# Key and query loads stacked into fewer transfers, and the first loads of a four-layer kernel put in another order

## The chip, the core and the metric

The kernel runs on one core of one Trainium2 chip. Its time is the device time of one execution in microseconds (us). The kernel before takes 3858.27 us, the median of 3 runs (3856.71 to 3861.03). The core has TensorE (PE, with its weight loads shown as PEld), VectorE (DVE), ScalarE (ACT), GpSimd (POOL) and SyncE (SP), and 16 DMA engines that all the engines' queues share. SP does nothing here but wait and start transfers.

## The reference, cut to what matters

Four layers work on one sequence x of 2048 tokens of 256 numbers. Each layer adds a cross attention over a context of 1601 rows of 192 numbers, and then a feed-forward part with routed experts.

```python
x = x + _L0_xattn_ref(_layernorm(x), ctx, Wq, bq, Wkv, bkv, Wo, bo)   # 16 heads of 16
x = x + _L0_ffn_ref(_layernorm(x), ...)        # 16 experts + shared, top 4
x = x + _L1_xattn_ref(...)                     # 16 heads of 16
x = x + _L1_ffn_ref(...)                       # 8 experts, top 2, gelu
x = x + _L2_xattn_ref(...)                     # 8 heads of 32
x = x + _L2_ffn_ref(...)                       # 8 experts, top 2, linear
x = x + _L3_xattn_ref(..., mask, ...)          # 16 heads of 16, the only one with the mask
x = x + _L3_ffn_ref(...)                       # 16 experts, top 2, gated

# one attention:
q, k, v = x @ Wq + bq, ctx @ Wk + bk, ctx @ Wv + bv      # split into heads
out = softmax(q @ k.T * scale) @ v
return out @ Wo + bo
```

All is float32. The scores are made of bfloat16 products: each query and key is split into three bfloat16 parts that add up to it, and six products of parts are summed.

## The kernel before, in words

**Stacks.** For a head of 16 numbers the six products are one matmul with 6 x 16 = 96 rows of contraction: `KS` (`k_stack`) holds for each head the key parts 0, 1, 0, 2, 1, 0 one under the other, each on 16 partitions, and `QS` (`q_stack`) the query parts that go with them, 0, 0, 1, 0, 1, 2. `PRODUCTS` is the list. For layer 2 with heads of 32 a stack is two halves of three parts each. A row 96 carries ones or the mask, rows 96 to 99 the negative row maxima.

**How a stack is filled.** The projections come out of PE with the channels on the partitions. ACT copies them, POOL or DVE splits them into three parts in a staging buffer `QP` (two of them, used in turn for keys and queries; a buffer is free when its store has landed), and SP stores them into DRAM (`k_parts`, `q_parts`, three parts of 256 channels each). From there `load_keys` and `load_queries` bring them back, each part onto its 16 (or 32) partitions of the stack. The heads are in four groups (g 0 to 3). `load_keys` issues six transfers of 200.1 KB for a group, 16 partitions x 4 heads x 1601 numbers. `load_queries` issues six of 64 KB and one for the row of ones, for a group and a chunk of 512 tokens.

**Maxima and scores.** Before the softmax of a group can start, the row maxima are needed: PE makes the scores of 128 tokens against 400 keys (L2259), DVE reduces them (L1524). Then in 13 steps over the keys PE makes the scores again (L2295), ACT takes the exponential (L1257), PE multiplies with the values (L2309), and maxima of the groups to come are made beside it. In steady state 16 groups of one layer (4 chunks x 4 groups) follow each other like this.

**The opening of layer 0.** SP loads x's first chunk, the context, all attention weights, then after a fence (all engines meet) the other chunks of x and the constant rows of the stack. ACT issues, beside it, the mask and the gate weights, with elements of 1 byte to 128 bytes. PE projects keys 0 to 2, turns the first tokens, and makes key 3 and queries 0 and 1 (`FIRST_UNITS`). When all their stores have landed, SP loads queries (0,0), keys of group 0, queries (0,1), keys of group 1; it stores the queries of groups 2 and 3, waits until that has landed, and loads queries (0,2). Then it stores keys 4 to 7 as they come. DVE turns the mask into numbers (`masks`). PE then works off 89 jobs of maxima (`side_prologue`), and after every second one a piece of the rest of the projections (`behind`): keys 4 to 7, values, the turning of the tokens ("turn"), queries. PE takes both in this one order, so a piece that waits holds back the maxima behind it.

**Layers 1 and 3** get their stacks during the feed-forward part before them: POOL issues the 24 key loads, one each time PE has finished a further unit (`load_keys(pool, ...)`), and SP stores and loads the first queries (`first_queries`). **Layer 2** gets them after layer 1's feed-forward part, from SP.

Lines to follow: L467 `load_keys`, L551 and L556 `load_queries`, L533 `store_query_parts`, L524 `store_key_parts`, L513 constant rows, L504 the attention weights but the key's, L608 x, L1100 to L1110 mask and gates on ACT's queue, L1139 ACT's copy of a key projection, L2324 "turn", L2155 the first half of a key projection on PE.

Of the kernel before, what the change touches and what calls it, by code (L numbers as in the profile page):

```python
# [5 lines left out]
T, D, S, DC = 2048, 256, 1601, 192  # L6
P = 128
# [30 lines left out]
PRODUCTS = [(0, 0), (1, 0), (0, 1), (2, 0), (1, 1), (0, 2)]  # L38
# [127 lines left out]
def build(nc, A, out):  # L166
# [5 lines left out]
    q_parts = nc.dram_tensor("q_parts", [3, D, T], bf16, kind="Internal").ap()  # L172
    k_parts = nc.dram_tensor("k_parts", [3, D, S], bf16, kind="Internal").ap()
# [8 lines left out]
    with ctx:  # L182
# [163 lines left out]
        s_wa = sem("s_wa")  # L346
        s_stat = sem("s_stat")
# [111 lines left out]
        def load_keys(eng, L, g, rows=(0, 6)):  # L459
# [11 lines left out]
        def _(sp):  # L471
# [12 lines left out]
            def load_attention_weights(L):  # L484
                a = ATT[L]
                dh, pw, hpg = a["dh"], a["pw"], a["hpg"]
                H = D // dh
                n = 0
# [5 lines left out]
                for dst, src in keys:  # L494
                    sp.dma_start(dst, src).then_inc(s_wk, 16)
                loads = [(WQ[:], A[f"wq{L}"].rearrange("(k p) n -> p k n", p=P)),
                         (WV0[:], A[f"wv{L}"][0:P, :]), (WV1[0:DC - P, :], A[f"wv{L}"][P:DC, :])]
                loads.append((WO[:], A[f"wo{L}"].rearrange("(a p) n -> p a n", p=P)))
                if L < 3:
                    loads += [(BQ[:], A[f"bq{L}"].rearrange("(m p) -> p m", p=P)),  # L500
                              (WV1[DC - P:DC - P + 1, :], A[f"bv{L}"].rearrange("(a n) -> a n", a=1)),
                              (BO[:], A[f"bo{L}"].partition_broadcast(P))]
                for dst, src in loads:
                    sp.dma_start(dst, src, allow_slow_non_contiguous=True).then_inc(s_wa, 16)  # L504

# [10 lines left out]
            def store_key_parts(u):  # L516
# [6 lines left out]
                dst = k_parts[:, m * P:(m + 1) * P, c * Q:c * Q + n].rearrange("r p t -> p r t")  # L523
# [3 lines left out]
            def store_query_parts(c, m):  # L527
# [4 lines left out]
                dst = q_parts[:, m * P:(m + 1) * P, c * Q:(c + 1) * Q].rearrange("r p t -> p r t")  # L532
# [8 lines left out]
            def load_queries(L, t, buf):  # L541
# [6 lines left out]
                if a["nsub"] == 1:  # L548
                    for row, (_, part) in enumerate(PRODUCTS):
                        src = q_parts[part].rearrange("(h d) t -> d h t", d=dh)[:, g * hpg:(g + 1) * hpg, cols]  # L550
                        sp.dma_start(dst[row * dh:(row + 1) * dh, :, :], src).then_inc(s_ql[buf], 16)  # L551
                else:
                    for row, (_, part) in enumerate(PRODUCTS):
                        src = q_parts[part].rearrange("(h d) t -> d h t", d=dh)[:, g * hpg:(g + 1) * hpg, cols]
                        r = row % 3
                        sp.dma_start(dst[r * dh:(r + 1) * dh, row // 3::2, :], src).then_inc(s_ql[buf], 16)  # L556
# [45 lines left out]
            sp.dma_start(X[:, 0:TPQ, :], x_chunks[0]).then_inc(s_x0, 16)  # L602
            sp.dma_start(C0[:], A["ctx_t"][0:P, :]).then_inc(s_ctx, 16)
            sp.dma_start(C1[0:DC - P, :], A["ctx_t"][P:DC, :]).then_inc(s_ctx, 16)
            load_attention_weights(0)
            fence(sp, fences)
            for c in range(1, NQ):
                sp.dma_start(X[:, c * TPQ:(c + 1) * TPQ, :], x_chunks[c]).then_inc(s_in, 16)  # L608
            load_constant_rows(0)
# [7 lines left out]
            load_keys(sp, 0, 0)  # L617
# [2200 lines left out]
```

## Time and profile before

| | |
|---|---|
| median of 3 runs | 3858.27 us (3856.71 to 3861.03) |
| the profiled execution | 3857.22 us, its span 3855.5 us, mean granted PE clock 0.966 |
| PE busy | 3615.5 us, 94% |
| DVE busy | 2536.7 us, 66% |
| ACT busy | 1931.5 us, 50% |
| POOL busy | 645.9 us, 17% |
| DMA | 171.33 MB, mean 44 GB/s |

A row of the stages (windows) view gives, for a stretch of the span, each engine's busy time and in brackets its instructions, the granted clock of PE, the mean busy share of the 16 DMA engines and what they moved. A row of the timeline is start, duration, engine, line, what is written from what, a count, and in square brackets the idle time just before it with what ended it. The duration of a transfer on SPq, ACTq or POOL is the time to issue it, from the first to the last of the count, and not the transfer itself.

### The profile page before, as it was taken

The numbers are of one execution on the slowest core, as the hardware profiler recorded it, in microseconds if no ns is written. First come the engines' busy times: TensorE is split into PE (matmuls) and PEld (weight loads), VectorE is DVE, ScalarE is ACT, GpSimd is POOL, SyncE is SP. The second block draws the span as 40 slices with busy tenths as digits, with TensorE's granted clock in tenths as the row PEclk, the third lists the DMA queues.
The fourth block names the chain that finished last, engine by engine and source line by source line (L and its number), as shares of the span: only waits on it lengthen the run. The fifth ranks groups of instructions, "written<-read, shape, count | busy, mean of one in ns | idle before, by whom it ended". The sixth has DMA issues, their size and how long they took to land. (4 is left out here: it accounts for less than half of the span.)

```text
span 3855.5 us, 50411 instructions
## 1 busy us (share of the span) xinstructions
PE 3615.5 (94%) x17554; PEld 1563.8 (41%) x17555; DVE 2536.7 (66%) x5373; ACT 1931.5 (50%) x2358; POOL 645.9 (17%) x940
## 2 busy tenths in 40 slices
PE   5999999799999999987997899999799999998996
PEld 2333333365533333325665333333433333332564
DVE  5888888456678888844223655553478888884523
ACT  3677777521147777762332444444203777777111
POOL 3200001200041010014221301010313001001242
PEclk8999999899999999998999899999799999999998
DMA  6300000123000000025001400000140000001144
GB/s 129 54 19 16 17 18 6 50 75 77 24 30 15 18 14 19 9 65 202 31 30 50 114 20 16 18 18 5 58 94 31 18 18 15 18 10 49 53 121 133
DMA packets 132653, 171.33 MB, mean 44 GB/s; under 512 B 38379, under 2 KB 106589, under 8 KB 130257
## 3 DMA queue, kind: packets, MB, share of 16 engines
q1 hardware_dynamic: 119280, 142.27, 13.2%
q0 software_dynamic: 10144, 26.08, 2.7%
q8 instruction: 126, 2.06, 0.2%
q14 instruction: 95, 0.77, 0.1%
q10 hardware_dynamic: 3008, 0.15, 0.1%
HBM read 131.27 MB, written 40.84 MB: 45 GB/s over the span
## 5 line engine op out<-in xcount | busy, mean ns | idle before, releaser
L1524 DVE TENSOR_REDUCE mx<-ps 128x1 f32<-128x400 f32 (+1 forms) x3584 | 1818.4, 566 | 495.3 <-PE ps L2259 483.9
L1257 ACT ACTIVATE probs<-ps,zero_col 128x1024 f32<-128x1024 f32 (+1 forms) x1040 | 1111.1, 1111 | 585.0 <-PE ps L2295 584.6
L2259 PE MATMUL ps<-k_stack,q_stack 97*128 97x400 bf16 (+1 forms) x3584 | 1076.5, 339 | 50.1 <-DMA k_stack<-k_parts 27.8
L2295 PE MATMUL ps<-q_stack,k_stack 100*128 100x512 bf16 (+2 forms) x3328 | 1056.9, 381 | 6.4 <-ACT probs L1257 6.4
L2309 PE MATMUL ps<-probs,v 128*32 128x512 f32 (+2 forms) x5824 | 891.5, 607 | 0.2 <-ACT probs L1257 0.2
L2259 PEld LDWEIGHTS ps<-k_stack,q_stack 97*128 97x128 bf16 x3584 | 290.4, 97 | 1049.2 <-DVE mx L1524 624.8
L1257 ACT ACTIVATE probs<-ps,mask_col 128x1024 f32<-128x1024 f32 (+1 forms) x416 | 439.5, 1110 | 158.6 <-PE ps L2295 158.6
L2295 PEld LDWEIGHTS ps<-q_stack,k_stack 100*128 100x128 bf16 (+2 forms) x3328 | 323.3, 100 | 345.0 <-ACT probs L1257 65.8
L2309 PEld LDWEIGHTS ps<-probs,v 128*32 128x32 f32 (+2 forms) x5824 | 140.1, 111 | 264.3 <-issue 248.8
L1674 DVE SCALAR_TENSOR_TENSOR x_res<-ps,comb,x_res 128x256 f32<-128x256 f32 x336 | 148.1, 479 | 63.0 <-PE ps L2559 57.5
L1325 ACT ACTIVATE h_t_s<-ps 128x512 f32<-128x512 f32 x80 | 47.8, 597 | 254.3 <-PE ps L2550 254.3
L2559 PE MATMUL ps<-w_up_s,h_t_s 128*128 128x256 f32 x640 | 164.4, 387 | 6.7 <-DVE x_res L1674 3.4
L932 POOL TENSOR_TENSOR o_t<-o_sum,recip_wide 128x512 f32<-128x512 f32 x32 | 40.7, 1273 | 713.4 <-DMA recip_wide<-row_recips 713.4
L2550 PE MATMUL ps<-xn_t,w_up_s 128*128 128x512 f32 x320 | 150.3, 592 | 0.6 <-ACT v L1151 0.6
L2640 PE MATMUL ps<-w_all,xn_t 128*128 x624 | 144.5, 385 | 3.7 <-ACT xn_t L1339 2.4
L934 POOL TENSOR_TENSOR o_sum<-o_sum,recip_wide 128x512 f32<-128x512 f32 x28 | 35.8, 1277 | 648.2 <-DMA recip_wide<-row_recips 648.2
L2619 PE MATMUL ps<-w_all,xn_t 128*128 x312 | 142.3, 599 | 1.6 <-SPq L776 1.6
L2559 PEld LDWEIGHTS ps<-w_up_s,h_t_s 128*128 128x128 f32 x640 | 114.2, 189 | 58.4 <-DVE x_res L1674 26.3
L2640 PEld LDWEIGHTS ps<-w_all,xn_t 128*128 128x128 f32 x624 | 118.2, 192 | 42.6 <-issue 28.0
L1339 ACT ACTIVATE xn_t<-ps,tile_bias 128x128 f32<-128x128 f32 x312 | 84.7, 382 | 100.0 <-PE ps L2631 99.8
L1369 ACT ACTIVATE silu_gate<-ps 128x320 f32<-128x320 f32 (+3 forms) x60 | 28.1, 468 | 197.0 <-PE ps L2715 99.7
L2573 PE MATMUL ps<-w_up_s,xn_t 128*128 128x512 f32 x256 | 120.0, 612 | 0.5 <-DVE x_res L1918 0.5
(293 smaller groups left out, 2715.0 us busy)
## 6 DMA issues: line engine op xcount, KB each, us to landing
q_stack<-q_parts SPq DMA_DIRECT2D x384, 64.0 KB, 2.2
q_parts<-qk_part SPq DMA_DIRECT2D x32, 384.0 KB, 2.5
w_up<-in_up SPq DMA_DIRECT2D x17, 704.0 KB
w_up_s<-in_expert SPq DMA_DIRECT2D x40, 256.0 KB, 2.7
k_stack<-k_parts SPq DMA_DIRECT2D x48, 200.1 KB, 7.1
k_stack<-k_parts POOLq DMA_DIRECT2D x48, 200.1 KB, 4.1
k_parts<-qk_part SPq DMA_DIRECT2D x24, 384.0 KB, 3.1
w_all<-in_up SPq DMA_DIRECT2D x8, 1024.0 KB, 12.6
```

The source lines that it names most:

```text
L1257: act.activation(PR[pair[0] % 4][0:r, :, :], PS[0:r, 2 * b:2 * b + 2, :], ACT.Exp, bias=mask_col[0:r, k:k + 1] if L == 3 else zero_col[0:r ...
L1339: last = act.activation(HB[:, q * P:(q + 1) * P], PS[:, 2 + q // 4, q % 4 * P:(q % 4 + 1) * P], ACT.Gelu, bias=BT[:, bass.ds(i, 1), q], sc ...
L1524: ins = dve.reduce_max(MX4[g % 2][:, u, c:c + 1], PS[:, bank, 0:CK[c]], AX.X)
L1674: dve.scalar_tensor_tensor(X[:, t, :], PS[:, b, 0:D], c, X[:, t, :], ALU.mult, ALU.add).then_inc(s_yf, 1)
L2259: last = mm(PS[:, bank, 0:CK[c]], QS[g][0:97, slot_of(j), qt * P:(qt + 1) * P], KS[0:97, (g * hpg + j) * nsub, CKO[c]:CKO[c] + CK[c]], sta ...
L2295: last = mm(PS[0:r, b + i, :], KS[0:rows, (g * hpg + jj) * nsub + sub, k * P:k * P + r], QS[g][0:rows, slot_of(jj) + sub, :], start=sub == ...
L2309: last = mm(PS[pw * jj:pw * jj + pw, 4, :], V[0:r, k, (g * hpg + jj) * pw:(g * hpg + jj) * pw + pw], PR[used[0] % 4][0:r, i, :], start=k = ...
L2550: last = mm(PS[:, n % 2, :], up[:, k, :], xnT[:, k, c * Q:(c + 1) * Q], start=k == 0, stop=k == 1)
L2559: mm(PS[:, 2 + yj[0] % 3, 0:D], HTS[n % 2][:, 0, i * P:(i + 1) * P], weight_slot(load)[1], start=True, stop=True).then_inc(s_y, 1)
L2573: last = mm(PS[:, n % 4, :], xnT[:, k, t * P:(t + 1) * P], WUS[i % 2][:, k * 512:(k + 1) * 512], start=k == 0, stop=k == 1)
L2619: last = mm(PS[:, half, :], XT1[par][:, k * P:(k + 1) * P], w1.rearrange("p a f -> p (a f)"), start=k == 0, stop=k == 1)
L2640: last = mm(PS[:, 4 + par, 0:D], HB[:, q * P:(q + 1) * P], w2.rearrange("p a f -> p (a f)"), start=q == 0, stop=q == NF // P - 1)
```

## The change

- **Stacked loads.** The channels of `wq`, `wk`, `bq`, `bk` are permuted on the way in (`heads_last`), so that in `q_parts` and `k_parts` the parts of a head group lie at one stride: number d of all heads of a half stands together. A load then brings several parts of the stack at once: for keys `(row, n, part)` is 3 times part 0, 2 times part 1, once part 2, and the repeat is a leading dimension of step 0 in the source (`to_broadcast`); for queries it is parts 0, 1, 2, then 0, 1, then 0, at a step. So a key group is 3 transfers in place of 6, a query group 4 in place of 7. In layer 2 a key group is 4 (three of one part and one of parts 0, 1, 2), a query group 6 in place of 7. The bytes are the same. The destination of a head group's rows is contiguous too now: 6404 numbers in a run.
- **POOL's key loads** for layers 1 and 3 are 12, one after every second unit.
- **First loads.** Context and key weights go first, x's first chunk after them, then the query weights; the constant rows go ahead of the other chunks of x. The value weights (`wv`, `wo`, `bv`, `bo`) go behind the keys of group 0. Mask and gates leave ACT's queue and stand on SP's behind queries (0,2). There is a semaphore of its own for the query weights.
- **masks()** moves from DVE to POOL, between the splitting of key 7 and of the first queries.
- **lead**: in layer 2 the first piece of `behind` comes after six maxima and not after two.

```diff
-PRODUCTS = [(0, 0), (1, 0), (0, 1), (2, 0), (1, 1), (0, 2)]
+KEY_LOADS = {1: [(0, 0, 3, 0, 0), (0, 3, 2, 1, 0), (0, 5, 1, 2, 0)],
+             2: [(0, 0, 1, 0, 0), (0, 1, 1, 0, 0), (0, 2, 1, 1, 0), (1, 0, 3, 0, 1)]}
+QUERY_LOADS = {1: [(0, 0, 3, 0, 1), (0, 3, 2, 0, 1), (0, 5, 1, 0, 0)],
+               2: [(0, 0, 2, 0, 1), (0, 2, 1, 0, 0), (1, 0, 1, 2, 0), (1, 1, 1, 1, 0), (1, 2, 1, 0, 0)]}
...
+        def stacked(parts, L, g, load):
+            dh, hpg = ATT[L]["dh"], ATT[L]["hpg"]
+            _, _, n, part, step = load
+            rows = parts[g // 2].rearrange("r (d h) s -> (r d) h s", h=P // dh)
+            heads = slice(g % 2 * hpg, (g % 2 + 1) * hpg)
+            if step == 0:
+                src = rows[part * dh:(part + 1) * dh, heads, :]
+                return src.unsqueeze(0).to_broadcast([n] + list(src.shape)) if n > 1 else src
+            return rows[part * dh:(part + n) * dh, heads, :]
...
-            for i in range(*rows):
-                part, _ = PRODUCTS[i]
-                src = k_parts[part].rearrange("(h d) s -> d h s", d=dh)[:, g * hpg:(g + 1) * hpg, :]
-                r, sub = (i, 0) if nsub == 1 else (i % 3, i // 3)
-                eng.dma_start(KS[r * dh:(r + 1) * dh, 4 * g + sub:4 * g + 4:nsub, :], src).then_inc(done, 16)
+            for load in KEY_LOADS[nsub][slice(*loads)]:
+                sub, r, n = load[0:3]
+                dst = KS[r * dh:(r + n) * dh, 4 * g + sub:4 * g + 4:nsub, :]
+                eng.dma_start(dst, stacked(k_parts, L, g, load)).then_inc(done, 16)
...
             load_queries(0, (0, 0), 0)
             load_keys(sp, 0, 0)
+            load_value_weights(0)
             load_queries(0, (0, 1), 1)
             load_keys(sp, 0, 1)
             store_query_parts(0, 1)
             wait_landed(qd)
             load_queries(0, (0, 2), 2)
+            sp.dma_start(mask_u8[:, 0:NK - 1], ...).then_inc(s_mask, 16)      # and 9 more
...
-                    for i in range(6 * NG):
-                        pool.wait_ge(s_y, results.at() + per_unit * (begin + i))
-                        load_keys(pool, L + 1, i // 6, (i % 6, i % 6 + 1))
+                    for i in range(3 * NG):
+                        pool.wait_ge(s_y, results.at() + per_unit * (begin + 2 * i))
+                        load_keys(pool, L + 1, i // 3, (i % 3, i % 3 + 1))
...
+                lead = TPQ if L == 2 else 0
                 for n, job in enumerate(jobs):
                     side(job)
-                    if n % every == every - 1 and behind:
+                    if n >= lead and n % every == every - 1 and behind:
```

The order of instructions shows the three places. First, SP's queue at the start of the program, before: key bias, query and value weights, then behind the fence (`s_fence`) the other three chunks of x, the constant rows and the first key stores.

```order
L495 DMA wk<-in_bk 1x256
L504 DMA wq<-in_wq 128x2x256
L504 DMA wv<-in_wv 128x256
L504 DMA wv<-in_wv 64x256
L504 DMA wo<-in_wo 128x2x256
L504 DMA bq<-in_bq 128x2x1
L504 DMA wv<-in_bv 1x256
L504 DMA bo<-in_bo 128x256
L608 DMA x_res<-in_x 128x4x256 [waits s_fence]
L608 DMA x_res<-in_x 128x4x256 x2
L513 DMA k_stack<-const_rows 1x16x1601 x4
L524 DMA k_parts<-qk_part 128x3x512 [waits s_kp] x3
```

The same stretch now, from the program's first transfer on.

```order
L618 DMA ctx_a<-in_ctx_t 128x1601
L619 DMA ctx_b<-in_ctx_t 64x1601
L505 DMA wk<-in_wk 128x256 [waits s_wpad]
L505 DMA wk<-in_wk 64x256
L505 DMA wk<-in_bk 1x256
L621 DMA x_res<-in_x 128x4x256
L508 DMA wq<-in_wq 128x2x256
L510 DMA bq<-in_bq 128x2x1
L534 DMA k_stack<-const_rows 1x16x1601 [waits s_fence]
L534 DMA k_stack<-const_rows 1x16x1601 x3
L626 DMA x_res<-in_x 128x4x256 x3
```

Four transfers with 0.59 MB (value weights, `wo`, `bv`, `bo`) have left the stretch ahead of the first key store, and the first chunk of x stands behind the key weights.

Second, SP's queue from the loads of queries (0,0) on, before (`s_kd`, `s_qd`: the key and query stores have landed; `s_kp`, `s_qp`: parts are ready to be stored).

```order
L551 DMA q_stack<-q_parts 16x4x512 [waits s_kd1,s_kd0,s_qd1]
L551 DMA q_stack<-q_parts 16x4x512 x5
L557 DMA q_stack<-const_rows 1x16x128
L467 DMA k_stack<-k_parts 16x4x1601 x6
L551 DMA q_stack<-q_parts 16x4x512 x6
L557 DMA q_stack<-const_rows 1x16x128
L467 DMA k_stack<-k_parts 16x4x1601 x6
L533 DMA q_parts<-qk_part 128x3x512 [waits s_qp]
L551 DMA q_stack<-q_parts 16x4x512 [waits s_qd1]
L551 DMA q_stack<-q_parts 16x4x512 x5
L557 DMA q_stack<-const_rows 1x16x128
L524 DMA k_parts<-qk_part 128x3x512 [waits s_kp] x3
```

The same place now, down to the value weights.

```order
L572 DMA q_stack<-q_parts 48x4x512 [waits s_kd1,s_kd0,s_qd1]
L572 DMA q_stack<-q_parts 32x4x512
L572 DMA q_stack<-q_parts 16x4x512
L573 DMA q_stack<-const_rows 1x16x128
L481 DMA k_stack<-k_parts 48x1x6404
L481 DMA k_stack<-k_parts 32x1x6404
L481 DMA k_stack<-k_parts 16x6404
L520 DMA wv<-in_wv 128x256
L520 DMA wv<-in_wv 64x256
L520 DMA wo<-in_wo 128x2x256
L520 DMA wv<-in_bv 1x256
L520 DMA bo<-in_bo 128x256
```

Queries (0,1) and keys of group 1 follow in the same form. Third, what stands on SP between the store of the queries of groups 2 and 3 and the stores of keys 4 to 6, now.

```order
L554 DMA q_parts<-qk_part 128x3x512 [waits s_qp]
L572 DMA q_stack<-q_parts 48x4x512 [waits s_qd1]
L572 DMA q_stack<-q_parts 32x4x512
L572 DMA q_stack<-q_parts 16x4x512
L573 DMA q_stack<-const_rows 1x16x128
L641 DMA mask_u<-in_mask 128x12x1
L643 DMA mask_u<-in_mask 65x1
L645 DMA mask_row_u<-in_mask 1x1601
L648 DMA gate_w<-in_gw 128x2x32 x3
L651 DMA gate_b<-in_gb 128x8
L648 DMA gate_w<-in_gw 128x2x32
L651 DMA gate_b<-in_gb 128x16
```

The stores of keys 4 to 7 now come behind ten more transfers.

## Rows read from the trace of the kernel before

**Rows 1.** Stages of 60 us: busy per engine, PE's clock, DMA share, GB/s.

```profile
0.00:60.00 60.00, 18.92 (x43) 8.76 (x45) 26.99 (x71) 17.09 (x35) 13.43 (x19) 0.75 0.80 153
...
180.00:240.00 60.00, 60.00 (x366) 20.22 (x359) 53.31 (x110) 46.13 (x45) 5.34 (x10) 1.00 0.07 18
```

**Rows 2.** Timeline, layer 0's opening: what PE waited for.

```profile
54.45 0.83 PE L2259 MATMUL ps<-k_stack,q_stack 97*128 97x401 bf16 x2 [27.80 <-DMA k_stack<-k_parts]
...
70.40 0.33 PE L2155 MATMUL ps<-ctx_a,wk 128*128 128x65 f32 x2
...
74.92 0.66 PE L2324 MATMUL ps<-ident,probs 128*128 128x128 f32 x4 [1.35 <-ACT qk_part L1140]
```

**Rows 3.** Timeline, ACT in layer 0's opening: the copies of keys 2, 5, 6, 7.

```profile
29.72 0.60 ACT L1139 ACTIVATE qk<-ps 128x512 f32<-128x512 f32 x1 [7.45 <-DMA k_parts<-qk_part]
...
66.08 0.60 ACT L1139 ACTIVATE qk<-ps 128x512 f32<-128x512 f32 x1 [3.81 <-DMA q_parts<-qk_part]
...
72.50 0.60 ACT L1139 ACTIVATE qk<-ps 128x512 f32<-128x512 f32 x1 [5.00 <-DMA k_parts<-qk_part]
...
74.53 0.23 ACT L1139 ACTIVATE qk<-ps 128x65 f32<-128x65 f32 x1 [0.60 <-DMA k_parts<-qk_part]
```

**Rows 4.** Transfers of the first 60 us: GB/s in 40 slices of 1.5 us; ACT's queue.

```profile
GB/s 0 138 195 149 401 200 158 160 257 241 282 334 348 198 39 95 153 139 128 59 5 0 196 196 132 33 30 133 103 190 132 128 130 134 122 150 237 130 128 135
...
q10 hardware_dynamic: 3008, 0.15, 4.2%
```

**Rows 5.** Timeline, SP's queue in layer 0's opening.

```profile
39.24 2.69 SPq L551 DMA_DIRECT2D q_stack<-q_parts  x6
41.97 0.52 SPq L557 DMA_DIRECT2D q_stack<-const_rows  x1
42.53 2.92 SPq L467 DMA_DIRECT2D k_stack<-k_parts  x6
...
65.99 2.65 SPq L551 DMA_DIRECT2D q_stack<-q_parts  x6
68.68 0.50 SPq L557 DMA_DIRECT2D q_stack<-const_rows  x1
69.22 8.85 SPq L524 DMA_DIRECT2D k_parts<-qk_part  x4
```

**Rows 6.** Stages: loads to 128 partitions, constant rows to one, key loads to 16.

```profile
18.00:20.00 2.00, 2.00 (x3) 0.59 (x3) 1.74 (x3) 0.16 (x1) 0.00 (x0) 1.00 1.17 350
20.00:22.00 2.00, 2.00 (x12) 1.45 (x11) 0.74 (x2) 1.79 (x4) 0.00 (x0) 1.00 1.28 81
120.00:122.00 2.00, 2.00 (x7) 0.79 (x6) 1.81 (x4) 1.11 (x1) 2.00 (x4) 0.50 1.06 120
```

**Rows 7.** The page's list of transfers: count, size, median us from issue to landing.

```profile
q_stack<-q_parts SPq DMA_DIRECT2D x384, 64.0 KB, 2.2
```

**Rows 8.** Timeline, ACT's queue: mask and gates (first and last of 10).

```profile
1.01 0.44 ACTq L1100 DMA_DIRECT2D mask_u<-in_mask  x1
...
8.13 0.84 ACTq L1110 DMA_DIRECT2D gate_b<-in_gb  x1
```

**Rows 9.** Timeline, POOL between key 7's split and the first query.

```profile
81.34 1.15 POOL L864 TENSOR_TENSOR qk<-qk,qk_part 128x512 f32<-128x512 f32 x1 [3.65 <-ACT qk_part L1238]
```

**Rows 10.** Timeline, PE in layer 2's opening; SP and PE in layer 3's.

```profile
2147.00 1.12 PE L2324 MATMUL ps<-ident,probs 128*128 128x128 f32 x4 [2.96 <-ACT probs L1189]
2147.91 0.88 PE L2259 MATMUL ps<-k_stack,q_stack 97*128 97x400 bf16 x2
...
2831.28 0.85 SPq L533 DMA_DIRECT2D q_parts<-qk_part  x1
2838.30 3.85 SPq L551 DMA_DIRECT2D q_stack<-q_parts  x6
2842.19 0.56 SPq L557 DMA_DIRECT2D q_stack<-const_rows  x1
...
2844.40 1.16 PE L2259 MATMUL ps<-k_stack,q_stack 97*128 97x401 bf16 x3 [8.37 <-issue]
```

More of the change, by code:

```diff
@@ L547, in load_queries @@
                 dst = QS[buf]
[L548 to L556, printed above, removed]
+                for load in QUERY_LOADS[a["nsub"]]:
+                    sub, r, n = load[0:3]
+                    rows = dst[r * dh:(r + n) * dh, sub::a["nsub"], :]
+                    sp.dma_start(rows, stacked(q_parts, L, g, load)[:, :, cols]).then_inc(s_ql[buf], 16)
                 sp.dma_start(dst[96:97, :, :], ones_row).then_inc(s_ql[buf], 16)
@@ L622, in _ @@
             load_queries(0, (0, 2), 2)
+            sp.dma_start(mask_u8[:, 0:NK - 1], A["mask"][:, 0:P * (NK - 1)].rearrange("a (k p) -> p (a k)", p=P),
+                         allow_slow_non_contiguous=True).then_inc(s_mask, 16)
+            sp.dma_start(mask_u8[0:KREM, NK - 1:NK], A["mask"][:, P * (NK - 1):S].rearrange("a p -> p a"),
+                         allow_slow_non_contiguous=True).then_inc(s_mask, 16)
+            sp.dma_start(mask_row_u8[:], A["mask"]).then_inc(s_mask, 16)
+            for L in range(4):
+                E = FFN[L]["E"]
+                sp.dma_start(GW[:, L], A[f"gw{L}"].rearrange("(k p) e -> p k e", p=P),
+                             allow_slow_non_contiguous=True).then_inc(s_gl, 16)
+                if L >= 2:
+                    sp.dma_start(GB[:, L, 0:E], A[f"gb{L}"].partition_broadcast(P)).then_inc(s_gl, 16)
             def first_queries(L):
@@ L854, in link, with masks @@
                 pool.wait_ge(s_const, n[0])
+            def masks():
+                pool.wait_ge(s_mask, 3 * 16)
+                link(pool.memset(mask_col[:], 0.0))
+                for r, lo, hi in ((P, 0, NK - 1), (KREM, NK - 1, NK)):
+                    link(pool.tensor_copy(mask_col[0:r, lo:hi], mask_u8[0:r, lo:hi]))
+                    link(pool.tensor_scalar(mask_col[0:r, lo:hi], mask_col[0:r, lo:hi], 1.0, -MASKED,
+                                            ALU.subtract, ALU.mult))
+                link(pool.tensor_scalar(mask_row, mask_row_u8[:], 1.0, -MASKED, ALU.subtract, ALU.mult))
             def clear_attention_weights(L):
@@ L965, in _ @@
                             split_keys(u, staged.take("key")[0])
+                        masks()
                     pool.wait_ge(s_qp, qp.at())
@@ L971, in _ @@
                 if L < 3:
-                    wa.step(16 * 7)
+                    wa.step(16 * 5)
                     pool.wait_ge(s_wa, wa.at())
@@ L1099, in _ @@
             rs = Count(s_rs)
[L1100 to L1110 removed]
+            wq = Count(s_wq)
             fence(act, fences)
@@ L1165, in scale_bias @@
             def scale_bias(scale):
+                wq.step(32 if wq.n < 96 else 16)
+                act.wait_ge(s_wq, wq.at())
                 act.activation(BQS[:], BQ[:], ACT.Copy, scale=scale).then_inc(s_bq, 1)
@@ L1598, in _ @@
                     if L == 0:
-                        masks()
                         for u in range(4):
@@ L2178, in project_next @@
                     wk.step(16 * (3 if L < 3 else 2))
-                    wa.step(16 * (7 if L < 3 else 4))
+                    wq.step(16 * (2 if L < 3 else 1))
+                    wa.step(16 * (5 if L < 3 else 3))
                     pe.wait_ge(s_wk, wk.at())
@@ L2350, in _ @@
                     wk.step(16 * 3)
-                    wa.step(16 * 7)
+                    wq.step(16 * 2)
+                    wa.step(16 * 5)
                     pe.wait_ge(s_wk, wk.at())
@@ L2764, in pairs_of_groups, with heads_last @@
         return np.swapaxes(m, 1, 2).reshape(D, D)
+    def heads_last(m, dh):
+        m = m.reshape(*m.shape[:-1], 2, P // dh, dh)
+        return np.swapaxes(m, -1, -2).reshape(*m.shape[:-3], D)
     def contraction_first(m, n):
```

76 lines of the change are left out of this document (33 added, 43 removed).

## The prediction

> **What bounds the kernel now.** I read the stages first. In the middle of an attention PE is busy without a gap (60.00 of 60 us, clock 1.00) and the DMA engines are 7% busy [rows 1]: there a cheaper transfer is worth nothing, since no engine waits for one. What the change touches can count only in the openings. In the first 60 us PE is busy 18.9 us, and the DMA engines 80% [rows 1]. So I read that opening in the timeline, engine by engine.
>
> PE stands still from 26.65 to 54.45 us, until the keys of group 0 have landed [rows 2]. That wait is a chain: ACT copies key 2 at 29.72, when the store of key 0 has landed and freed its staging buffer [rows 3]; the last stores land and SP starts to load at 39.24; it issues seven query and six key loads until 45.45 [rows 5]. After that there is a second chain, which decides the end of the opening. The store of the queries of groups 2 and 3 stands in the queue behind group 1's keys and lands at 65.99, and only then ACT can copy key 5, at 66.08; SP loads queries (0,2), stores key 4 at 69.22 [rows 5], ACT copies key 6 at 72.50 and key 7 at 74.53 [rows 3], and PE, which has waited 1.35 us, goes on at 74.92 with the turning of tokens [rows 2]. From there the opening runs on work, not on transfers. So the question is when PE reaches this instruction in the changed kernel.
>
> **Durations of transfers.** The rate goes with the destination: x to 128 partitions runs at 350 GB/s, the constant rows to one partition at 81, the key loads to 16 partitions at 120, each with the DMA engines full [rows 6]. The best slice has 401 GB/s [rows 4], which is 25 GB/s for each of 16 engines.
>
> **Step 1, the first loads.** Ahead of the first key store stand 0.59 MB less (value weights, wo, bv, bo; shapes in the order), 1.7 to 4.9 us at 350 to 120 GB/s; I take 2.0, since these go to 128 partitions. The small packets of ACT's queue, 4.2% of 16 engines for 60 us [rows 4], are 2.5 us. The engines are full where rows 6 look into this time (shares 1.17 and 1.28), so both come off: ACT copies key 2 at 25.2 and the loads start at 39.24 - 4.5 = 34.7. That the first chunk of x comes later, and the constant rows before the other chunks, changes nothing in the sum of the bytes ahead of that store; bounds of this step 0 (if the chain on PE and DVE sets the store) and 7.4 us.
>
> **Step 2, issue.** Seven query loads take 2.69 + 0.52 = 3.2 us [rows 5], four 1.8. Their 0.46 MB at 120 to 350 GB/s land in 1.3 to 3.9 us, I take 2.3: key data of group 0 flow from 38.0.
>
> **Step 3, the stacked key loads.** This is the term on which all depends and the trace does not show it. A group is 1.23 MB (6 x 200.1 KB). Bounds: 3.1 us, with all engines at their best (401 GB/s), and 56 us, if few engines work at the 7.5 GB/s each that the key loads show (120 / 16). Two of the three new loads have a source whose leading dimension is the repeat, 3 or 2, and a destination of 48 or 32 partitions. A transfer that is dealt out to the engines along the leading dimension of both sides can be dealt to three and to two of them only. I take this as the likeliest: engines 0 and 1 then carry 205 KB of the first load, 205 KB of the second and 12.8 KB of the third, 0.423 MB at 25 GB/s = 16.9 us, against 10.2 us before (1.23 MB at 120). The rate of 25 and not 7.5, because what held the key loads to 120 is by rows 6 the few partitions written at a time, and runs of 12.8 KB in place of 3.2 can't cost more. The only repeated source in rows 6 is the constant rows', with 16 repeats, and the engines were full with it: a repeat as such doesn't confine, but this row can't show what three do.
> The Trainium skill, DMA: Bandwidth & Descriptors, section on why a DMA increments its semaphore by 16, says that the engine count is the largest one up to 16 that divides the slowest dimension of both access patterns, and its rules for authors warn of a leading zero-stride broadcast of c copies; by it the counts are 3, 2 and 16, and no run shown here tests that.
>
> Landing adds 2.2 us [rows 7]: keys of group 0 are there at 38.0 + 16.9 + 2.2 = 57.1, against 54.45. The 4.5 us of step 1 are gone.
>
> **Step 4, what is queued behind.** All later transfers on SP's queue use the loaded engines too: value weights (37 KB each at 25 GB/s, 1.5 us), queries (0,1) (28 KB, 1.1), group 1's keys (16.9), the query store (25 KB, 1.0). So it lands at 54.9 + 20.5 + 2.2 = 77.6, against 65.99. The value weights land 1.5 us behind group 0's keys, and PE asks for them only some maxima and a key projection later: no wait, and about 1 us if that cover is gone.
>
> **Step 5, SP's new duties.** Then 1.8 us of query loads and the ten transfers of mask and gates. On ACT's queue they took from 1.01 to 8.97 us, 8.0 us [rows 8]. ACT had nothing to do then; on SP the store of key 4 stands behind them. Bounds 4.5 us (ten at 2.69 / 6, what a query load takes to issue [rows 5]) and 8.0; I take 8.0, the row of the same transfers. Key 4 is stored at 77.6 + 1.8 + 8.0 = 87.4, against 69.22. As before ACT copies key 6 3.3 us after it and key 7 2.0 us later [rows 3, 5], and PE turns 0.4 us after that: 93.1, against 74.92, **18.2 us later**.
> PE takes its jobs in order, so the maxima behind can't fill this: it reaches the first half of key 7 (70.40, 16 us after its first maximum [rows 2]) at 73 us and stops there until key 5 is copied at 77.7.
>
> **Step 6, masks on POOL.** DVE loses work in a time in which it waits for PE's first maximum anyway: nothing. The long one of the six instructions is 1601 numbers on one partition; POOL's 512 on each partition take 1.15 us [rows 9], so 3.6 us, and POOL stands idle 3.65 us at that place. I take nothing; bounds 0 and +3.6, should the queries' split have to wait for all of it. SP issues the mask about 10 us before POOL gets there.
>
> **Step 7, the other openings.** Layer 2: PE waits 2.96 us for ACT with two maxima done; four more, twice 0.88 us by the next row, fit in [rows 10]: -1.5 us (bounds 0, -2.9). Layer 3: queries are stored at 2831.28, SP loads them from 2838.30 to 2842.75, and PE starts at 2844.40 after 8.37 us [rows 10]; four loads in place of seven save 1.8 us. But POOL's stacked key loads then run beside that store on two or three engines, and packets of 12.8 KB can hold it up: 0 to +8 us; I take 0. Layer 1's key loads come one after every second expert unit and expert weights are loaded four ahead: nothing, at most what I allow for layer 3. Layer 2's key loads have no repeat and are covered.
>
> **Sum.** +18.2 - 1.5 - 1.8 = +14.9 us. The profiled execution took 3857.22 us (span 3855.5 and 1.7 around it), 1.1 us under the median of the runs: 3872.1 for it, 3873 for a median.
>
> **Rivals.**
> (a) *The stacks use all 16 engines.* For it: the repeat of 16 in rows 6, and nothing in the trace against it. Then 1.03 MB to 48 and 32 partitions at 300 GB/s and 0.2 MB at 120 take 5.1 us. First maximum 38.0 + 5.1 + 2.2 = 45.3; query store landed at 43.1 + 2.0 + 1.5 + 5.1 + 1.3 + 2.2 = 55.2; SP 1.8 + 8.0: key 4 stored at 65.0, PE turns at 70.7, 4.2 us earlier. With step 7: -7.5 us, 3851; with the ten transfers at 4.5 us, 3847. This is the other side of zero.
> (b) *The stacks move as slowly as before* (destination-bound at 120 GB/s whatever their shape). Query store landed at 48.2 + 2.0 + 1.5 + 10.2 + 1.3 + 2.2 = 65.4; +9.8, +5.7: PE turns at 80.9, +6.0; with step 7 +2.7: 3861. The change then does little of what it says.
> (c) *Few engines, and something else gets stuck too*: the engine's rate is under 25 GB/s, or in layer 3 the query store waits its full 8 us behind POOL's packets. Each 5 GB/s less costs 4.2 us in each of two groups. From 3886 up.
>
> **Chances.** Forecast (3864 to 3886) 0.62; (a) 0.22; (b) 0.08; (c) 0.08. The forecast's own range is 3864 to 3886: 16.9 could be 14 or 20 us twice, step 5 3.5 us less, step 1 3 us either way. To hold 8 in 10 the range must reach into (a) and (c): 3850 to 3888. A measurement of this kernel can tell 0.2%, 7.7 us, from no change. Faster by more: half of (a) and a little, 0.12. Within: the rest of (a), (b), and the bottom of the forecast, 0.24. Slower: 0.64.
>
> **What would show it.** In the profile after: PE's first maximum (layer 0) at 57 if the forecast is right, at 45 for (a), 50 for (b); ACT's copy of key 5 waiting for the query store until about 77; the DMA share in these 40 us far under 1 with about 50 to 75 GB/s, where before it was full at 120; the ten transfers on SP about 8 us long, and PE's turn at about 93. Issue to landing of key loads at 15 us and more, on POOL's queue too. ACT's key 2 at 25 would show step 1. I am wrong if the share stays near 1 in the key loads, or if the attention's steady stages change by more than 1 us each.

## The result and the profile after

The changed kernel took 3899.9 us (median of 4 runs, 3895.5 to 3902.6), the kernel before 3859.65 us beside it (3856.7 to 3864.5): a ratio of 1.0102, 95% interval [1.0084, 1.0119]. That is slower, as forecast, but by 40 us and not by 15, and outside the range of 3850 to 3888. The profiled execution has a span of 3899.6 us against 3855.5.

The same stages of 60 us as in [rows 1], with one more between them: length; busy us of PE, of its weight load, of DVE, ACT and POOL, each with its number of instructions; PE's granted clock; share of the 16 DMA engines; GB/s.

```profile
0.00:60.00 60.00, 13.10 (x32) 5.98 (x33) 20.03 (x60) 16.48 (x33) 13.45 (x19) 0.71 0.60 136
60.00:120.00 60.00, 40.45 (x139) 22.34 (x140) 29.86 (x58) 13.86 (x36) 24.80 (x27) 0.75 0.25 72
180.00:240.00 60.00, 57.69 (x319) 19.03 (x323) 48.12 (x97) 40.75 (x40) 2.76 (x6) 0.91 0.08 20
```

The DMA engines are busy for 0.60 of the first stage, where it was 0.80: they stand idle while PE waits for them. And the stage from 180 to 240 us, in which I had said that a transfer decides nothing, has lost 2.3 us of PE's work and a tenth of its clock.

PE's timeline, at the places of [rows 2, 10] and at two new ones (start, duration, engine, line, tiles; in brackets the idle time ahead and what ended it):

```profile
62.16 0.83 PE L2280 MATMUL ps<-k_stack,q_stack 97*128 97x401 bf16 x2 [39.63 <-DMA k_stack<-k_parts]
83.91 0.69 PE L2175 MATMUL ps<-ctx_a,wk 128*128 128x65 f32 x2 [8.71 <-ACT qk_part L1170]
95.57 1.11 PE L2345 MATMUL ps<-ident,probs 128*128 128x128 f32 x4 [6.94 <-ACT qk_part L1170]
182.31 0.85 PE L2280 MATMUL ps<-k_stack,q_stack 97*128 97x401 bf16 x2 [4.20 <-DMA q_stack<-m_parts]
934.02 0.83 PE L2280 MATMUL ps<-k_stack,q_stack 97*128 97x401 bf16 x2 [9.56 <-issue]
2193.16 1.11 PE L2345 MATMUL ps<-ident,probs 128*128 128x128 f32 x4 [1.06 <-ACT probs L1221]
2890.10 1.16 PE L2280 MATMUL ps<-k_stack,q_stack 97*128 97x401 bf16 x3 [17.86 <-issue]
```

The first maximum comes at 62.16, not 54.45; the turn of tokens at 95.57, not 74.92 (+20.7). The waits of 4.20 us (row maxima of group 1, layer 0) and 9.56 us (layer 1's opening) are new; layer 3's went from 8.37 to 17.86; layer 2's from 2.96 to 1.06. Counted at the same instruction in both traces, the lag is 20.7 at the turn, 23.0 ahead of the wait of 4.20 us, 31.8 behind it and until layer 0's attention ends, 43.4 in layer 1's first steady stretch (1133.23 against 1089.87), 45.0 at layer 2's opening, 40.3 when its attention ends, 36.2 ahead of layer 3's wait, 45.8 behind it (2943.80 against 2898.04) and 44.3 at the last wait.

ACT's copies of keys 2, 5 and 6, which answer to [rows 3]:

```profile
23.72 0.60 ACT L1169 ACTIVATE qk<-ps 128x512 f32<-128x512 f32 x1 [5.66 <-DMA k_parts<-qk_part]
82.77 0.60 ACT L1169 ACTIVATE qk<-ps 128x512 f32<-128x512 f32 x1 [14.62 <-DMA q_parts<-qk_part]
93.85 0.60 ACT L1169 ACTIVATE qk<-ps 128x512 f32<-128x512 f32 x1 [9.65 <-DMA k_parts<-qk_part]
```

SP's queue, which answers to [rows 5]; the duration of a row is the time that the issue took, not the transfer:

```profile
33.27 1.30 SPq L572 DMA_DIRECT2D q_stack<-q_parts  x3
...
35.16 2.02 SPq L481 DMA_DIRECT2D k_stack<-k_parts  x3
...
39.64 18.77 SPq L572 DMA_DIRECT2D q_stack<-q_parts  x3
...
59.06 1.91 SPq L481 DMA_DIRECT2D k_stack<-k_parts  x3
61.02 0.48 SPq L554 DMA_DIRECT2D q_parts<-qk_part  x1
82.68 1.28 SPq L572 DMA_DIRECT2D q_stack<-q_parts  x3
...
84.60 0.58 SPq L641 DMA_DIRECT2D mask_u<-in_mask  x1
...
90.05 9.39 SPq L545 DMA_DIRECT2D k_parts<-qk_part  x4
```

Three query loads, 1.30 us of issue at 33.27, take 18.77 at 39.64: SP itself is stuck behind group 0's keys until 58.41, 3.7 us before PE can use them. So group 1's keys are issued only at 59.06, and the query store lands at 82.6.

Three windows of stacked key loads: group 0's (first) and group 1's (last) with little beside them, and in the middle group 1's with other packets beside:

```profile
46.00:54.00 8.00, 0.00 (x0) 0.00 (x0) 0.00 (x0) 1.11 (x3) 0.00 (x0) 0.50 0.19 58
66.00:72.00 6.00, 6.00 (x25) 3.54 (x24) 4.91 (x11) 1.53 (x4) 2.92 (x3) 1.00 0.17 72
70.00:78.00 8.00, 5.20 (x23) 2.98 (x20) 5.36 (x11) 0.00 (x0) 0.77 (x1) 1.00 0.14 56
```

A share of 0.19 is three engines of 16, and 58 GB/s over three is 19 GB/s for each. With group 1 each engine did more: 72 GB/s at 0.17 (2.7 engines) is 26, and 56 GB/s at 0.14 (2.2 engines) is 25. Nothing here shows why group 0's went slower.

### The profile page after: what moved, and what is told of

The parts are those of the page before. It is cut to its first block and busy times, and to the rows that moved or that the text cites. A ratio compares the mean times of both kernels' runs of the same rounds, so it can differ in the third digit from the quotient of the medians.

```text
span 3899.6 us, 50207 instructions
## 1 busy us (share of the span) xinstructions
PE 3619.3 (93%) x17554; PEld 1568.1 (40%) x17555; DVE 2535.3 (65%) x5367; ACT 1933.3 (50%) x2358; POOL 643.5 (17%) x922
```

## The experiments

Theory F: a leading dimension of 3 or 2 confines a load to 3 or 2 engines, and what is behind it on the queue waits. Its rivals: W, wide transfers or long packets are slow by themselves; O, the new order of first loads and the transfers moved to SP cost the time. All ratios are to the kernel before. (The texts below speak of ten mask and gate transfers, as the prediction and [rows 8] do: they are nine, three and six.)

**1. The same transfers with the repeat inside.**

```diff
-  src.unsqueeze(0).to_broadcast([n] + list(src.shape))          # 3 x 16 rows
+  src.unsqueeze(1).to_broadcast([dh, n] + list(src.shape)[1:])  # 16 rows, 3 times each
```

> The changed kernel, with the same three key loads to 48, 32 and 16 partitions, the same bytes and the same 12.8 KB runs, but in layers 0, 1 and 3 the repeat stands inside the source (16 rows, each read 3 or 2 times in a row) instead of ahead of it; the stacked rows are then in another order, so the queries of these layers go in six transfers. Theory F (few engines: a leading dimension of 3 or 2 confines a load to 3 or 2 DMA engines): key loads fill the engines again, first maximum of layer 0 at about 47 us instead of 62, the turn of tokens at about 74 instead of 95.6, the new gaps at 182, 934 and the 9.5 us more at 2890 go; total 3848 to 3858. Rival W (wide or long packets: a transfer to 48 partitions with 12.8 KB runs is slow by itself, whatever the order of its source): nothing changes, about 3900. Rival O (the new order of the first loads and the ten mask and gate transfers on SP are what costs): at most the keys come earlier, the turn stays at about 90 and the total at 3880 or more.

Measured: 3865.95 us, ratio 1.0012 [1.0003, 1.0022]. PE and two windows of the key loads:

```profile
49.53 0.83 PE L2288 MATMUL ps<-k_stack,q_stack 97*128 97x401 bf16 x2 [27.00 <-DMA k_stack<-k_parts]
...
76.64 1.11 PE L2353 MATMUL ps<-ident,probs 128*128 128x128 f32 x4 [10.53 <-ACT qk_part L1178]
```
```profile
39.00:47.00 8.00, 0.00 (x0) 0.00 (x0) 1.94 (x17) 6.26 (x13) 0.00 (x0) 0.50 0.89 166
47.00:55.00 8.00, 5.47 (x13) 2.67 (x14) 2.61 (x6) 2.00 (x5) 0.00 (x0) 0.56 1.12 202
```

The engines are full again, at 166 to 202 GB/s (other loads included) instead of 58, for the same bytes in the same number of key loads to the same 48, 32 and 16 partitions in the same runs. Nothing but the order of the source's dimensions changed, the order of the stacked rows with it, and the queries go in six loads, which cost time in run 11. 34 us of the 40 go with it. W falls, and F holds. The Trainium skill (DMA: Bandwidth & Descriptors, rules for kernel authors) warns of just this leading broadcast; this pair of runs agrees with it.
But the total is 8 us above the range that F gave, 3848 to 3858: what else holds it is the subject of runs 5 to 10.

**2. Six key loads**, to 16 partitions each, still in runs of 12.8 KB.

```diff
-  dst = KS[r * dh:(r + n) * dh, 4 * g + sub:4 * g + 4:nsub, :]
-  eng.dma_start(dst, stacked(k_parts, L, g, load)).then_inc(done, 16)
+  if nsub == 1:
+      for i in range(n):
+          dst = KS[(r + i) * dh:(r + i + 1) * dh, 4 * g + sub:4 * g + 4:nsub, :]
+          eng.dma_start(dst, stacked(k_parts, L, g, (0, 0, 1, load[3], 0))).then_inc(done, 16)
```

> The changed kernel, with the key loads alone undone: in layers 0, 1 and 3 six transfers to 16 partitions in place of three, still 12.8 KB runs; stacked query loads, order of the first loads, masks on POOL and the lead stay. F: first maximum at about 50, turn at about 78, total 3850 to 3860, within 5 us of the kernel with the repeat inside. W: 3850 to 3860 too, since nothing is wide any more, so only the comparison with the other kernel tells F from W. O: 3880 or more.

Measured: 3859.94 us, 0.9994 [0.9985, 1.0004], 6.0 us under run 1 where F gave 5 at most; run 11 puts the price of six query loads at 4.4. The first maximum is at 48.77, the turn at 76.03 after 8.51 us. So the stacked key loads cost 40 us, all that the change lost, and the rest of the change is worth nothing in sum. Two waits are still longer than before the change, 3.57 us in layer 1 (0.56 before) and the one ahead of the turn. That one seems to cost twice:

```profile
75.00:80.00 5.00, 3.46 (x13) 2.33 (x13) 2.02 (x4) 2.40 (x9) 4.08 (x9) 0.50 0.11 38
80.00:85.00 5.00, 5.00 (x9) 2.18 (x10) 1.49 (x4) 0.67 (x2) 4.76 (x4) 0.50 0.20 52
```

Behind it the granted clock is 0.50, the lower level of 1.2 GHz; before the change, where PE waited 1.35 us there, it was 1.00 from 70 us on. The turn is 1.1 us later than before, the next common wait, at 106.27 against 101.44, 4.8 us.

**3. Six key loads in layer 0 alone**; POOL's stay stacked.

```diff
-  if nsub == 1:
+  if L == 0:
```

> The changed kernel, with the key loads undone in layer 0 alone (SP's loads); POOL's stacked key loads of layers 1 and 3 stay. F: layer 0 gets back about 32 us and the gaps at the openings of layers 1 and 3 stay (about 9.5 us each over before): total 3865 to 3872, some 12 to 18 us above the kernel with six loads everywhere. If POOL's loads cost nothing and the later gaps only followed from layer 0: the same as with six loads everywhere. O: 3880 or more.

Measured: 3872.02 us, 1.0029 [1.0019, 1.0038]; waits of 10.13 us at 903 and 16.27 us at 2853. POOL's stacked loads cost 12 us against run 2, layer 0's 28. The wait at 182 us is gone here, as in runs 1 and 2; it comes in every version that stacks layer 0's keys (4.20, 3.70 in run 4, 3.72 in run 8, 2.28 in run 12).

**4. The changed kernel with mask and gate transfers back on ACT's queue**, all nine, ahead of the fence.

```diff
-  sp.dma_start(mask_u8[:, 0:NK - 1], ...)    # and the eight behind it, on SP
+  act.dma_start(mask_u8[:, 0:NK - 1], ...)   # on ACT, then fence(act, fences)
```

> The changed kernel, stacked loads and all, but the three mask and seven gate transfers are issued by ACT ahead of the first fence, as before the change (the masks are still computed on POOL). F: SP saves the 5.4 us they take ahead of the store of key 4, the first loads lose some us to their small packets: turn of tokens at 90 to 93 instead of 95.6, total 3894 to 3899. O: the opening falls back to about 75 us for the turn, total about 3875 or less.

Measured: 3900.78 us, 1.0101 [1.0084, 1.0118]: no gain. ACT copies key 2 at 27.77 instead of 23.72, so these small packets hold the first loads up by 4.05 us, and the first maximum comes at 66.69. That eats what SP saves: PE turns at 96.93, where F gave 90 to 93. O falls as the main cause; what the order of the first loads costs is run 10.

**5. Run 2, with mask and gates ahead of the wait for the query store.**

```diff
   store_query_parts(0, 1)
+  (three mask and six gate transfers)
   wait_landed(qd)
   load_queries(0, (0, 2), 2)
-  (three mask and six gate transfers)
```

> The kernel with six key loads, and the ten mask and gate transfers moved on SP from behind the third query loads to ahead of the wait for the query store, a time in which SP stood idle for 15 us. In the kernel with six key loads the store of key 4 was issued at 70.3 us, and PE, after a wait of 8.5 us, went on at half clock (granted clock 0.50 from 75 to 85 us); it turned tokens at 76.0 but was 4.8 us behind the kernel before at 106 us. Theory S (SP's ten transfers cost their 5.1 us on the path, and the wait that they lengthen costs a second time by the clock): key 4 stored at 65.2, turn at about 71, the wait about 3.5 us, the clock stays at 1.00 or falls later and shorter; layer 0 ends 7 to 9 us earlier, total 3851 to 3854. Rival (the transfers only change places: they delay the query loads and the key store in the queue as much): total 3858 to 3861.

Measured: 3859.75 us, 1.0003 [0.9993, 1.0012], the same as run 2. SP:

```profile
46.37 0.42 SPq L559 DMA_DIRECT2D q_parts<-qk_part  x1
46.84 0.49 SPq L644 DMA_DIRECT2D mask_u<-in_mask  x1
47.37 15.08 SPq L646 DMA_DIRECT2D mask_u<-in_mask  x1
```

The second of them takes 15.08 us to issue, so six gates still stand ahead of key 4 when the query store lands. Key 4 is stored at 67.72, 2.6 us earlier and not 5.1, and PE turns at 73.9 after 6.17 us, which is neither theory's figure, and the total gains nothing. I missed that an issue can block.

**6. Run 5, with POOL's key loads paced singly**, one of 200 KB behind each expert unit, as before the change.

```diff
-  for i in range(3 * NG):
-      pool.wait_ge(s_y, results.at() + per_unit * (begin + 2 * i))
+  for i in range(6 * NG):
+      pool.wait_ge(s_y, results.at() + per_unit * (begin + i))
```

> The kernel with six key loads and the mask and gate transfers early, and POOL's key loads in layers 1 and 3 one transfer of 200 KB behind each expert unit, as before the change, instead of three, two and one behind every second. Theory P (a burst of 400 to 600 KB on POOL's queue holds up SP's query store, which landed after 9.4 us instead of 4.2 in the opening of layer 1, and PE waits 3.6 us that it didn't before): the gap before the first maximum of layer 1 falls under 1 us, that of layer 3 from 9.7 to 8.4 or less, total 4 to 6 us under the kernel with masks early alone, 3845 to 3849, faster than both kernels. Rival (it is the packets of 12.8 KB that hold up the query store, not the burst): the gaps stay, same total as with masks early alone.

Measured: 3850.99 us, 0.9980 [0.9971, 0.9990], 8.8 us under run 5, more than the 4 to 6 of theory P. Layer 1's wait of 1.81 us is gone, layer 3's went from 10.08 to 8.36 us. From trace to trace layer 1's opening gives 1.6 us and layer 3's 5.1; 2.8 come in the last feed-forward part, where the two kernels are the same. From SP's second query store of layer 1 to the loads that wait for it: 9.4 us with bursts (SP's queue in run 2, first), 4.5 us now (second).

```profile
893.19 0.58 SPq L559 DMA_DIRECT2D q_parts<-qk_part  x1
902.62 2.61 SPq L577 DMA_DIRECT2D q_stack<-q_parts  x3
```
```profile
894.73 0.58 SPq L559 DMA_DIRECT2D q_parts<-qk_part  x1
899.21 2.38 SPq L577 DMA_DIRECT2D q_stack<-q_parts  x3
```

In the changed kernel the same store, issued at 920.76, held its loads until 935.57.

**7. Run 6 without the lead in layer 2.**

```diff
-  lead = TPQ if L == 2 else 0
+  lead = 0
```

> The kernel of the run before it in this call, without the lead of four maxima in layer 2. Theory L (the lead takes away PE's wait of about 3 us and with it the fall of the clock behind it: before the change 2180 to 2200 us stood at 0.82, with the lead at 1.00): 3 to 5.5 us slower. Rival (only the wait of 1.5 us that I predicted): 1 to 2 us slower. If the gain of layer 2 came from its stacked loads: no change.

Measured: 3857.36 us, 0.9993 [0.9984, 1.0003], 6.4 us over run 6, though the intervals touch. In the profiled executions PE's wait is 2.96 us again, and the stretch from layer 2's opening to its end 3.1 us longer. The lead is worth 3 to 6 us; I had taken 1.5. (The profiled execution, 3850.2, is one of the three quick ones of ten, so the trace can't say where a median 6.4 us higher comes from.) In that stretch the clock was 0.82 from 2180 to 2200 before the change, and 1.00 in run 6.

```profile
2180.00:2200.00 20.00, 19.08 (x72) 6.05 (x73) 9.89 (x19) 7.79 (x7) 10.12 (x15) 0.82 0.71 163
```
```profile
2180.00:2200.00 20.00, 18.70 (x82) 6.14 (x83) 12.44 (x25) 9.01 (x9) 13.87 (x19) 1.00 0.74 182
```

But without the lead it was 0.95 there, so how much of the 3 to 6 us is clock these runs don't settle.

**8. The changed kernel, stacked, with the edit of run 5.**

> The changed kernel, stacked loads on few engines and all, with the ten mask and gate transfers moved ahead of the wait for the query store. F (few engines hold back everything behind them): the small transfers now lie behind group 1's keys in the queue and run beside the last of them; SP stores key 4 about 5.4 us earlier, turn at about 90 instead of 95.6, total 3893 to 3896. If SP's issue is blocked again, as between 39.6 and 58.4 us, where three query loads took 18.8 us to issue, the ten end only when the queue drains and nothing is gained: 3898 to 3901.

Measured: 3900.74 us, 1.0110 [1.0093, 1.0127]. The second mask transfer took 18.76 us to issue, until 81.6. Key 4 was stored 2.8 us earlier, and no gain can be measured: the second of the two cases.

**9. Run 6 with the gates behind the store of key 7**, masks still early.

```diff
   store_query_parts(0, 1)
   (three mask transfers)
-  (six gate transfers)
   wait_landed(qd)
   ...
   for u in range(4, 8):
       store_key_parts(u)
   wait_landed(kd)
+  (six gate transfers)
```

> The kernel with six key loads, masks and gates early and POOL paced singly, and now only the three mask transfers stand ahead of the wait for the query store; the six gate transfers go behind the store of key 7, where SP stood idle for 10 us. In the kernel before it SP's second mask transfer took 14.8 us to issue, until the query store landed at 61.9, and the gates then 2.9 us, so key 4 was stored at 67.1, hardly earlier than before the change (69.2). Theory S: key 4 stored at 64.1, turn at 70.6 instead of 73.7, PE's wait there 3.5 us instead of 6.5 and less of it at half clock; total 3 to 5 us lower, 3846 to 3848. Rival (the clock, not the wait, sets it: PE's first long wait has already used up the clock's budget): the turn comes earlier but layer 0 ends where it did, 3850 to 3852.

Measured: 3846.79 us, 0.9963 [0.9951, 0.9974]. Key 4 is stored at 64.31, PE turns at 71.08 after 4.59 us. Times and total are as theory S has them, but the clock isn't: it stands at 0.50 from 70 to 80 us all the same.

**10. Run 9 with the old order of the first loads.**

```diff
+  sp.dma_start(X[:, 0:TPQ, :], x_chunks[0]).then_inc(s_x0, 16)
   (context)
-  load_key_weights(0); (chunk 0 of x); load_query_weights(0)
+  load_attention_weights(0)
   fence(sp, fences)
-  load_constant_rows(0)
   (chunks 1 to 3 of x)
+  load_constant_rows(0)
   ...
   load_keys(sp, 0, 0)
-  load_value_weights(0)
```

> The kernel with gates behind the key stores, but the first loads in their old order: the first chunk of x, context and all attention weights, value weights too, ahead of the fence, chunks of x ahead of the constant rows. Theory R (bytes ahead of the first key store are on the path while the engines are full): ACT copies key 2 some 3.5 to 6 us later (24 to 29), first maximum from 48 to 51 or 53, but the value weights no longer stand between the keys of groups 0 and 1, which gives 2 to 3 us back at the query store; total 1 to 4 us higher than the kernel before it. Rival (order is without effect on the end): the same within 1 us.

Measured: 3842.57 us, 0.9956 [0.9939, 0.9972]: 4.2 us under run 9, where I had expected 1 to 4 over it (the intervals overlap; it is surely not slower). SP and PE of run 10:

```profile
45.15 0.42 SPq L559 DMA_DIRECT2D q_parts<-qk_part  x1
...
63.23 8.82 SPq L550 DMA_DIRECT2D k_parts<-qk_part  x4
```
```profile
49.35 0.83 PE L2286 MATMUL ps<-k_stack,q_stack 97*128 97x401 bf16 x2 [25.84 <-DMA k_stack<-k_parts]
...
69.99 1.12 PE L2351 MATMUL ps<-ident,probs 128*128 128x128 f32 x4 [4.50 <-ACT qk_part L1176]
```

ACT copies key 2 at 26.14 instead of 24.57 and the first maximum is 1.3 us later, but with no value weights between the keys of groups 0 and 1 the query store is issued 1.0 us earlier and key 4 stored 1.1 us earlier. PE turns 1.1 us earlier. This is the fastest version tried: 17 us under the kernel before, 57 us under the changed one.

**11. Run 9 with six query loads** in place of the stacked ones, in all layers.

```diff
-  for load in QUERY_LOADS[a["nsub"]]:
+  for load in [(s, r + i, 1, p + i * st, 0)
+               for s, r, m, p, st in QUERY_LOADS[a["nsub"]] for i in range(m)]:
```

> The kernel with gates behind the key stores, but every query load of every layer as six transfers and one of ones, as before the change. Theory Q (SP's issue of 0.45 us each is on the path in the openings of layers 0 and 3): first maximum 1.4 us later, key 4 stored 2 to 3 us later, layer 3's gap before its first maximum 1.8 us longer; total 3 to 6 us higher. Rival (the loads' bytes, not their issue, decide): within 1 us.

Measured: 3851.15 us, 0.9980 [0.9971, 0.9990], 4.4 us over run 9, though the intervals touch. The size fits, the places only in part (the trace is of the quickest execution, 3844.5 us): key 4 is stored 1.4 us later, but layer 3's wait is 8.52 us against 8.37, not 1.8 longer. Six loads took 3.96 us there, three take 3.64:

```profile
2830.96 3.64 SPq L577 DMA_DIRECT2D q_stack<-q_parts  x3
```

**12. Stacked in layer 0 alone**: the changed kernel with POOL's loads as in run 6.

```diff
-  if nsub == 1:          # condition of run 2
+  if L in (1, 3):
```

> The changed kernel, with the key loads of layers 1 and 3 undone (POOL: one transfer of 200 KB behind each expert unit, as before) and SP's stacked loads of layer 0 as they are; it is the complement of the kernel that undid layer 0 alone. F: layer 0 keeps its 32 us, the gaps at 934 (9.6 us) and the 9.5 us more at 2890 go: total 3878 to 3884. If POOL's loads cost nothing of their own: 3900.

Measured: 3880.46 us, 1.0052 [1.0036, 1.0069]. The waits of layers 1 and 3 are as before the change (8.18 us at 2868). POOL's part is 19 us: 12 for the few engines (run 3) and 9 for bursts (run 6) make about that.

## Why the prediction was wrong

The direction was right, and so was the mechanism in layer 0 up to the turn; its reach behind the turn and into layers 1 and 3 was put at nothing, and so the size was not: +14.9 us, measured +44.1 from profile to profile. By its steps:

1. **First loads.** Forecast 4.5 us earlier, measured 6.0 (23.72 against 29.72). The split was the wrong way round: ACT's queue gave 4.05 (run 4), not 2.5, and the order of the rest 1.6 (run 10), not 2.0. At the loads' start it was 6.0 as well (33.27 against 39.24).
2. **Issue.** Group 0's queries and keys as forecast (the queries are 0.40 MB and not 0.46, since the row of ones is 4 KB: 0.3 us). Behind them SP was stuck for 18.8 us, and no step of mine had that. For step 4 I take it as a matter of little weight, since three busy engines could not have carried group 1's keys sooner; no run tests that.
3. **Stacked key loads.** The engines counted (3 and 2) fit the shares of the windows, and run 1 shows that the leading dimension confines them. The first maximum was forecast at 57.1 and came at 62.16. Mis-sized is the rate for group 0: 25 GB/s for each engine against the 19 measured. 19 instead of 25 in the same 0.423 MB is 22 us and not 16.9, which is the size of the error, though the loads started 1.4 us earlier than forecast, so that over 1 us is left. Group 1's went at 25 to 26, as forecast. The forecast also had the value weights behind group 0's keys: in the trace the engines are full from 38 to 44 us (share 1.01, 167 GB/s), so it seems that they ran beside them.
4. **Queue behind.** Query store forecast at 77.6, landed at 82.6: step 3's 5 us, carried on. From the first maximum to that landing I had 20.5 us, and it took 20.4.
5. **SP's nine transfers** took 5.45 us (84.60 to 90.05), near the lower of my bounds and not the upper that I took. So PE turned 20.7 us late, and the forecast of 18.2 for that instruction is as near as it is by luck: two errors of opposite sign, +5.0 in step 3 and -2.6 here.
6. **Masks on POOL.** Not tried alone. No wait for them shows in the profile after.
7. **What failed.** Of the 29 us between forecast and measurement 2.5 lie at the turn. The rest comes from two sentences, less what layer 2 gave. First, behind the turn: "From there the opening runs on work, not on transfers." The lag grew by 11.1 us between the turn and the end of layer 0's attention. SP issued the keys of groups 2 and 3 at 135.69, and the row maxima of group 1, stored at 169.78, were held behind them:

```profile
135.69 3.97 SPq L481 DMA_DIRECT2D k_stack<-k_parts  x6
140.16 16.50 SPq L572 DMA_DIRECT2D q_stack<-q_parts  x3
...
169.78 0.32 SPq L609 DMA_DIRECT2D m_parts<-m_part  x1
180.33 0.26 SPq L614 DMA_DIRECT2D q_stack<-m_parts  x1
```

That store and its load lay 1.5 us apart for group 0 and 10.5 here. PE then waited 4.20 us, and the lag grew by 8.8 us there; where layer 0's keys aren't stacked (runs 1 to 3) the wait is absent. The remaining 7 us of the 11.1 are the work that PE did at a lower clock, as far as the windows show it, and smaller gaps: 0.50 from 90 to 100 us, where it was 1.00 before, and 0.74 from 180 to 200. No run prices the clock by itself. I counted queued transfers only up to the turn, and waits only at their own length.

Second, in step 7: "0 to +8 us; I take 0" for layer 3, and "nothing, at most what I allow for layer 3" for layer 1. Layer 3's wait grew by 9.5 us and layer 1's, from nothing, to 9.56. From the end of layer 0's attention into layer 1 the lag grew 11.6 us, over layer 3's opening 9.5 (36.2 to 45.8). That is the mechanism of rival (c), which I gave 0.08: once the forecast's own mechanism holds, a query store behind POOL's packets on few engines is no separate accident but its consequence, in two more layers. The two belonged to one case, at about 3894 by my own sum with the 9.56, the 9.5 and the 1.8 us in it (an estimate).
The small terms: layer 2's attention gained 4.7 us, not 1.5. Another 4.1 us come in layer 2's feed-forward part, which neither my sum nor any run accounts for; the traces of all changed versions have them, and with a single trace of the kernel before I can't tell cause from chance. Of layer 3's 1.8 us for fewer query loads nothing reaches PE: the issue is indeed shorter (1.30 us for three at 2881.17, 3.85 for six before), but the query store ahead of it holds SP for 13.7 us where it was 7.0. And in run 9, without that delay, three took 3.64 us and the wait is 8.37 us, as before the change.

Rival (a), all engines, would have had the mechanism right without the repeat ahead: runs 1 and 2 are that kernel, but at 3866 and 3860, not 3847 to 3851. Its rate of 300 GB/s was too high (166 to 202 in run 1's windows; the first maximum came at 49.5 and 48.8, not 45.3). POOL's bursts and the clock behind a wait are what it lacked besides.

## What to carry to other kernels

Before transfers are merged, look at the leading dimension of both sides: fewer, larger loads lose all if it is 3. Putting the 16 rows outside and the repeat inside fills the engines, but it orders the stacked rows anew, and here the queries lost their own stacking by it (4.4 us in run 11). A queue on few engines delayed the transfers behind it, and those of another queue too; so follow each later transfer on these engines through all stages that share the pattern, and put the same mechanism at its price in every one of them. A transfer moved to where an engine seems idle can still be on the path: move it behind the last one that somebody waits for (run 9), not just earlier (run 5).

## What the runs showed of the hardware

- The order of dimensions in the source alone took a load to 48 partitions from 58 GB/s at a share of 0.19 to 166 to 202 GB/s at a full share (0.89 to 1.12, with other loads in the window).
- One engine moved 19 GB/s in packets of 12.8 KB with group 0's keys (58 GB/s on three) and 25 to 26 with group 1's (56 GB/s at a share of 0.14).
- Loads on few engines delay a transfer that is not confined to few, from another queue too: SP's query store to its loads in layer 1 takes 14.8 us beside POOL's stacked loads, 9.4 beside bursts of single ones, 4.5 when these are paced.
- Issuing a transfer can block: 18.77 and 16.50 us for three query loads behind stacked keys, and 11 to 15 us for a mask transfer of single bytes behind key loads with all engines at work (runs 5, 6, 7, 9, 10 and 11; 18.76 us in run 8, stacked), while two dozen transfers ahead of it were issued without a stop. What limit it meets isn't settled here.
- After a wait of 8.5 us PE ran for about 10 us more at a granted clock of 0.50; in run 9 a wait of 4.59 us was followed by the same from 70 to 80 us, in run 10 one of 4.50 us by 0.66 for 5 us and 1.00 then. Executions of one kernel spread over 6 to 14 us (run 6: 3846.8 to 3853.1; run 11: 3844.5 to 3858.1), so a single profile can be several us off its median.
